# Two VectorE instructions of a softmax joined into one scalar_tensor_tensor, under a list scheduler

## The chip, the cores and the metric

The kernel runs on the 8 cores of one Trainium2 chip. Cores work in pairs on one of four sequences; nothing passes between them on the chip. The metric is the device time of the slowest core in microseconds. Each core has TensorE (PE: matmuls), VectorE (DVE), ScalarE (ACT), GpSimd (POOL) and SyncE (SP: issues transfers here). A transfer is a DMA.

## What is computed

`x` has the shape 4 x 4096 x 1024. The reference, cut to its core:

```
def attn(x):                       # x is layernormed
    out = gelu(x); on = out / |out|
    sim = on @ on.T, strictly causal, max over the past
    fam = w * max_sim + (1 - w) * (on @ ema)
    gate = 1 - alpha + alpha * exp(-tau * fam)
    return out * gate[..., None]

def ffn(x):                        # x is layernormed, tokens n
    gate = softmax(xt @ gate_w.T, axis=-1)                    # 8 experts
    base = xt @ weight.T                                      # 1024 x 1024
    t = einsum('nh,erh->ner', xt, lora_U)                     # rank 16
    lora = einsum('ne,eor,ner->no', gate, lora_V, t)
    return base + lora / 16

x = x + attn(layernorm(x))
x = x + ffn(layernorm(x))
```

## The kernel before

Each core owns 16 tiles of 128 tokens (`NSLOT`) and sees 32 key tiles. Three stages overlap in time.

The key stage loads tiles, takes mean and variance, applies gelu (L422) and the norm, makes the normalised tile in bf16 (L446, GpSimd), transposes it on TensorE (L455) into two PSUM banks and casts both halves into `kT` (L461 on VectorE, L465 on ScalarE). The similarity stage (`qk_slot`) multiplies one own tile with blocks of up to 512 keys (L507), two blocks at a time, and VectorE takes the maximum of each block (L528). The third stage is the feed-forward one. For tile `m` it holds, in `g_slot` and the two functions that the print below shows:

- `g_slot`: gating and residual (L612), statistics (L618, L619, L621), and two ScalarE steps for the inverse deviation (L623, L627).
- `ffn_part1`: L643 and L647 make the layernormed tile `z2tok`; L657 transposes it; L664 (VectorE) and L667 (ScalarE) cast the halves into `kT`. Then L678 and L681 make, over 8 chunks, the low-rank product (128 columns) and the gate's logits (8 columns) in one bank. L684 and L687 make the big product, 16 matmuls of 512 columns into two banks. The softmax runs over L694 (maximum), L697 (exponential, on ScalarE), L701 (sum), L704 (reciprocal), L707 (scaling the 8 exponentials) and L710 (the low-rank product times the 8 gates, each over 16 columns, into `tgb`).
- `ffn_part2`: L721 transposes `tgb`, L725 (ScalarE) copies it, L728 and L730 add the low-rank part to the big product, L733 and L736 add the result to `h`. Two tiles at a time are written out from SyncE's queue.

PSUM has eight banks: `ps0` to `ps4` go round for L507, L684 and L687 (two for each tile), `ps6` and `ps7` for the transposes (L455, L657, L721), and `ps5` alone is for L678 and L681 of every tile:

```
    pspools = {"big": [0, 1, 2, 3, 4], "tr": [6, 7], "one": [5]}
```

No engine's order is written out. `P.op` records operations with what they read and write, and a cost in ns. `P.schedule` is a list scheduler: an operation's priority is its cost plus the largest priority of those that need its result, and at each step the operation that can start earliest by these costs is taken, the higher priority first. So the costs set the order of each engine's instructions and nothing else:

```
            o.prio = o.cost + o.bonus + m
...
                if best is None or st < best[0] or \
                        (st == best[0] and nprio < best[1]):
                    best = (st, nprio, e, oid)
```

Of the kernel before, what the change touches and what calls it, by code (L numbers as in the profile page):

```python
# [12 lines left out]
ALU = mybir.AluOpType  # L13
# [190 lines left out]
def build_program():  # L204
# [57 lines left out]
    rinv2 = sb("rinv2", [128, 2], F32)  # L262
    gexp2 = sb("gexp2", [128, 2, 8], F32)
# [10 lines left out]
    def psalloc(pool="big"):  # L274
        lst = pspools[pool]
        i = lst[psidx[pool] % len(lst)]
        psidx[pool] += 1
        return pst[i], ("ps", i)
# [9 lines left out]
    p = P()  # L288
# [8 lines left out]
         reads=[("ident",)], writes=[("identf",)], cost=200.0)  # L297
# [3 lines left out]
         writes=[("xbuf", 1)], dma=True)  # L301
# [3 lines left out]
         reads=[("srow",)], writes=[("crow",)])  # L305
    p.op("scalar", lambda e: e.activation(crow[:, 5:6], srow[:, 1:2], AF.Exp, scale=-1.0),
         reads=[("srow",)], writes=[("crow",)])
    p.op("scalar", lambda e: e.activation(crow[:, 6:7], srow[:, 2:3], AF.Exp, scale=-1.0),
         reads=[("srow",)], writes=[("crow",)])
    p.op("vector", lambda e: e.tensor_scalar(crow[:, 5:6], crow[:, 5:6], 1.0, None, ALU.add),  # L310
         reads=[("crow",)], writes=[("crow",)])
    p.op("vector", lambda e: e.reciprocal(crow[:, 2:3], crow[:, 5:6]),
         reads=[("crow",)], writes=[("crow",)])
    p.op("vector", lambda e: e.tensor_scalar(crow[:, 3:4], crow[:, 2:3], -1.0, 1.0, ALU.mult, ALU.add),
         reads=[("crow",)], writes=[("crow",)])
    p.op("vector", lambda e: e.tensor_scalar(crow[:, 6:7], crow[:, 6:7], 1.0, None, ALU.add),
         reads=[("crow",)], writes=[("crow",)])
    p.op("vector", lambda e: e.reciprocal(crow[:, 7:8], crow[:, 6:7]),
         reads=[("crow",)], writes=[("crow",)])
    p.op("vector", lambda e: e.tensor_tensor(crow[:, 0:1], crow[:, 4:5], crow[:, 7:8], ALU.mult),  # L320
         reads=[("crow",)], writes=[("crow",)])
    p.op("vector", lambda e: e.tensor_scalar(crow[:, 6:7], crow[:, 7:8], -1.0, 1.0, ALU.mult, ALU.add),
         reads=[("crow",)], writes=[("crow",)])
    p.op("vector", lambda e: e.tensor_tensor(crow[:, 1:2], crow[:, 4:5], crow[:, 6:7], ALU.mult),
         reads=[("crow",)], writes=[("crow",)])
# [4 lines left out]
         reads=[("ones",), ("crow",)], writes=[tC])  # L330
    p.op("vector", lambda e: e.tensor_copy(constcols[:, :], psC[:, 0:8]),
         reads=[tC], writes=[("constcols",)])
# [7 lines left out]
         reads=[("zt", 0)], writes=[("xbuf", 0), ("tiny",)])  # L340
    p.op("vector", lambda e: e.tensor_scalar(tiny[:, 0:1], tiny[:, 0:1], 1e-24, None, ALU.max),
         reads=[("tiny",)], writes=[("tiny",)])
    p.op("scalar", lambda e: e.activation(tiny[:, 1:2], tiny[:, 0:1], AF.Ln),
         reads=[("tiny",)], writes=[("tiny",)])
    p.op("scalar", lambda e: e.activation(tiny[:, 2:3], tiny[:, 1:2], AF.Exp, scale=-0.5),
         reads=[("tiny",)], writes=[("tiny",)])
    p.op("vector", lambda e: e.tensor_scalar(embf, emarow, tiny[:, 2:3], None, ALU.mult),
         reads=[("zt", 0), ("tiny",)], writes=[("ktok", 0)])
    psE, tE = psalloc("big")
    fns = []  # L350
    for c in range(NCHUNK):
# [5 lines left out]
         reads=[tE], writes=[("emaf",)])  # L357

    p.op("vector", lambda e: e.tensor_copy(gwbf, wstage[0:8, 1, :]),
         reads=[("xbuf", 1)], writes=[("ktok", 1)])  # L360
    psG, tG = psalloc("big")
    fns = []
    for c in range(NCHUNK):
# [7 lines left out]
        reads=[tG], writes=[("gwTb",)])  # L371

    p.default_bonus = 0.0
    for c in range(NCHUNK):
        p.op("scalar", lambda e, c=c: e.dma_start(
            wstage[:, c % 2, :], wtd[c * 128:(c + 1) * 128, :]),
            writes=[("xbuf", c % 2)], dma=True, cost=2500.0)
        p.op("vector", lambda e, c=c: e.tensor_copy(wTb[:, c, :], wstage[:, c % 2, :]),
             reads=[("xbuf", c % 2)], writes=[("wTb",)], cost=600.0)
# [3 lines left out]
        writes=[("xbuf", 0)], dma=True)  # L383
    p.op("vector", lambda e: e.tensor_copy(
        uTb[:, :, :], wstage[:, 0, :].rearrange("p (c j) -> p c j", c=8)),
        reads=[("xbuf", 0)], writes=[("uTb",)])
    p.op("scalar", lambda e: e.dma_start(wstage[:, 1, :], vpd),
         writes=[("xbuf", 1)], dma=True)
    p.op("vector", lambda e: e.tensor_scalar(vPb[:, :], wstage[:, 1, :], 0.0625, None, ALU.mult),
         reads=[("xbuf", 1)], writes=[("vPb",)])  # L390
# [250 lines left out]
    def ffn_part1(m):  # L641
        buf = m % 2
        p.op("vector", lambda e: e.scalar_tensor_tensor(  # L643
            rtmp16[:, m:m + 1], mv2[:, m, 0:1], -1.0, rstd16[:, m:m + 1],
            ALU.mult, ALU.mult),
            reads=[("mv2", m), ("rstd16", m)], writes=[("rtmp16", m)], cost=90.0)
        p.op("scalar", lambda e: e.activation(  # L647
            z2tok[:, buf, :], h[:, m, :], AF.Identity,
            bias=rtmp16[:, m:m + 1], scale=rstd16[:, m:m + 1]),
            reads=[("h", m), ("rtmp16", m), ("rstd16", m)], writes=[("z2", buf)],  # L650
            cost=700.0, act_set="lnexp")
        pa, ta = psalloc("tr")
        pb, tb = psalloc("tr")
        fns = []
        for c in range(NCHUNK):
            ps = pa if c < 4 else pb
            fns.append(lambda e, c=c, ps=ps: e.matmul(  # L657
                ps[:, (c % 4) * 128:(c % 4) * 128 + 128],
                z2tok[:, buf, c * 128:(c + 1) * 128], ident[:, :],
                start=(c % 4 == 0), stop=(c % 4 == 3), skip_group_check=True))  # L660
        p.op("tensor", fns, reads=[("z2", buf), ("ident",)], writes=[ta, tb],
             cost=900.0)
        col = 128 * m
        p.op("vector", lambda e: e.tensor_copy(  # L664
            kT[:, 0:4, col:col + 128], pa[:, :].rearrange("p (c f) -> p c f", c=4)),
            reads=[ta], writes=[("kT", m, 0)], cost=660.0)
        p.op("scalar", lambda e: e.copy(  # L667
            kT[:, 4:8, col:col + 128], pb[:, :].rearrange("p (c f) -> p c f", c=4)),
            reads=[tb], writes=[("kT", m, 1)], cost=580.0)
        z2toks = [("kT", m, 0), ("kT", m, 1)]  # L670
        psA, tA = psalloc("big")
        psB, tB = psalloc("big")
        psT, tT = psalloc("one")
        fnsT = []
        fnsAB = []
        for c in range(NCHUNK):
            lhs = kT[:, c, 128 * m:128 * m + 128]
            fnsT.append(lambda e, c=c, lhs=lhs, psT=psT: e.matmul(  # L678
                psT[:, 0:128], lhs, uTb[:, c, :],
                start=(c == 0), stop=(c == 7), skip_group_check=True))  # L680
            fnsT.append(lambda e, c=c, lhs=lhs, psT=psT: e.matmul(  # L681
                psT[:, 128:136], lhs, gwTb[:, c, :],
                start=False, stop=(c == 7), skip_group_check=True))
            fnsAB.append(lambda e, c=c, lhs=lhs, psA=psA: e.matmul(  # L684
                psA[:, :], lhs, wTb[:, c, 0:512],
                start=(c == 0), stop=False, skip_group_check=True))
            fnsAB.append(lambda e, c=c, lhs=lhs, psB=psB: e.matmul(  # L687
                psB[:, :], lhs, wTb[:, c, 512:1024],
                start=(c == 0), stop=False, skip_group_check=True))
        p.op("tensor", fnsT, reads=z2toks + [("uTb",), ("gwTb",)],  # L690
             writes=[tT], cost=1350.0)
        p.op("tensor", fnsAB, reads=z2toks + [("wTb",)],
             writes=[tA, tB], cost=3550.0)
        p.op("vector", lambda e, psT=psT: e.reduce_max(  # L694
            nmax2[:, buf:buf + 1], psT[:, 128:136], axis=AX, negate=True),
            reads=[tT], writes=[("nmax", buf)])
        p.op("scalar", lambda e, psT=psT: e.activation(  # L697
            gexp2[:, buf, :], psT[:, 128:136], AF.Exp, bias=nmax2[:, buf:buf + 1]),
            reads=[tT, ("nmax", buf)], writes=[("gexp", buf)],
            cost=310.0, act_set="lnexp")  # L700
        p.op("vector", lambda e: e.reduce_sum(  # L701
            ssum2[:, buf:buf + 1], gexp2[:, buf, :], axis=AX),
            reads=[("gexp", buf)], writes=[("ssum", buf)])
        p.op("vector", lambda e: e.reciprocal(  # L704
            rinv2[:, buf:buf + 1], ssum2[:, buf:buf + 1]),
            reads=[("ssum", buf)], writes=[("rinv", buf)])
        p.op("vector", lambda e: e.tensor_scalar(  # L707
            gexp2[:, buf, :], gexp2[:, buf, :], rinv2[:, buf:buf + 1], None, ALU.mult),
            reads=[("gexp", buf), ("rinv", buf)], writes=[("gexp", buf)])
        p.op("vector", lambda e, psT=psT: e.tensor_tensor(  # L710
            tgb[:, buf, :].rearrange("p (ee r) -> p ee r", ee=8),
            psT[:, 0:128].rearrange("p (ee r) -> p ee r", ee=8),
            gexp2[:, buf, :].unsqueeze(2).broadcast_to([128, 8, 16]),
            ALU.mult),
            reads=[tT, ("gexp", buf)], writes=[("tg", buf)], cost=280.0)
        return (m, buf, psA, tA, psB, tB, psT, tT)

    def ffn_part2(st):
# [28 lines left out]
    for m in range(NSLOT):  # L747
        st = ffn_part1(m)
        if prev is not None:
            ffn_part2(prev)  # L750
        prev = st
# [55 lines left out]
```

How the kernel before makes its waits and increments, by code:

```python
                def section(eng, ename=ename):  # L172
                    clk = {}
                    for oid in self.sched[ename]:
                        o = ops[oid]
                        waits = {}
                        for pid in o.preds:
                            p_ = ops[pid]
                            if clk.get(p_.semn, 0) < p_.semv:
                                if waits.get(p_.semn, 0) < p_.semv:
                                    waits[p_.semn] = p_.semv
                        if o.dma and o.semv > 16:
                            prev = o.semv - 16
                            if clk.get(o.semn, 0) < prev and \
                                    waits.get(o.semn, 0) < prev:
                                waits[o.semn] = prev
                        for s, v in sorted(waits.items()):
                            eng.wait_ge(sems[s], v)
                            if clk.get(s, 0) < v:
                                clk[s] = v
                        inst = None
                        for fn in o.fns:
                            inst = fn(eng)
                        if inst is not None:
                            inst.then_inc(sems[o.semn], 16 if o.dma else 1)
                    if ename == "gpsimd":
                        for s in QPOOL["sync"] + QPOOL["scalar"]:
                            if totals.get(s, 0) > 0:
                                eng.wait_ge(sems[s], totals[s])
```

## Time and profile before

| | us |
|---|---|
| time before, median of 2 runs | 391.79 (391.3 to 392.28) |
| the profiled execution | 392.92 |
| its span on the slowest core (core 1) | 391.3 |
| spans of the eight cores | 385.0 to 391.3 |
| busy in the span: PE / DVE / ACT / POOL | 244.5 / 236.9 / 148.0 / 60.7 |

The span runs from the first to the last instruction of a core. The profiled execution's own time stands 1.6 us above the span. Busy times of engines overlap, so they don't add up to the span. The mean granted clock of TensorE was 0.946 of full speed on this core and 0.945 to 0.950 on the others.

### The profile page before, as it was taken

Reading aid. Unit: us, or ns where it says so; the run is one execution under the profiler, and the core shown is the slowest. Engines: PE = TensorE matmul, PEld = TensorE weight load, DVE = VectorE, ACT = ScalarE, POOL = GpSimd, SP = SyncE. Lnnn points to the kernel's source line nnn. Section 1 sums busy time; section 2 is a strip of 40 time slices with the busy share of each in tenths; the row PEclk is TensorE's granted clock in tenths of the full one; section 3 lists DMA queues with packets and bytes.
Section 4 is the critical chain, followed back from the end, with each engine's and each line's share of the span. In section 5 each row is a group of like instructions: output and inputs, shape, how many; then the busy total and the mean of one; then the engine's idle time right before and its main releaser. Section 6 shows DMA issues by size and latency. Waiting matters only on the chain.

```text
span 391.3 us, 5559 instructions; the slowest of 8 cores (385.0 to 391.3 us)
## 1 busy us (share of the span) xinstructions
PE 244.5 (62%) x1762; PEld 135.1 (35%) x1762; DVE 236.9 (61%) x537; ACT 148.0 (38%) x252; POOL 60.7 (16%) x38
## 2 busy tenths in 40 slices
PE   0100000166567777788588797889879688887781
PEld 0000000064234444455234354445445344443540
DVE  0222177755857677648634656459889796877533
ACT  1100009755665571731731065103354344243410
POOL 0000000563242325115013013210000000000000
PEclk9999999999688899999969999999989999999895
DMA  7866510236033333113303030333330222022222
GB/s 218 281 201 182 133 73 0 107 107 216 1 107 109 111 107 108 54 55 109 107 2 107 1 109 1 109 107 110 107 108 7 104 110 107 6 104 107 109 110 108
DMA packets 11665, 39.30 MB, mean 100 GB/s; under 512 B 1259, under 2 KB 2283, under 8 KB 11636
## 3 DMA queue, kind: packets, MB, share of 16 engines
q1 hardware_dynamic: 6528, 25.17, 18.2%
q10 hardware_dynamic: 5108, 13.78, 11.1%
q8 instruction: 15, 0.25, 0.2%
q14 instruction: 14, 0.11, 0.1%
HBM read 30.55 MB, written 8.39 MB: 100 GB/s over the span
## 4 chain that ended last, share of the span: by engine, by line
PE 37%; DVE 21%; issue 15%; ACT 12%; DMA 11%; DVEq 1%; ACTq 0%; SPq 0%
PE ps L507 22%; DMA xbuf<-wt 4%; PE ps L455 3%; PE ps L684 3%; PE ps L687 3%; ACT xbuf L422 3%; DVE st L411 3%; ACT h L422 2%; DVE colbuf L528 2%; ACT L422 2%; PE ps L678 2%; PE ps L657 2%; DMA ztile<-ema 2%; DMA xbuf<-x 2%; DMA xbuf<-gw 2%
## 5 line engine op out<-in xcount | busy, mean ns | idle before, releaser
L507 PE MATMUL ps<-kT 128*128 128x512 bf16 (+3 forms) x640 | 136.7, 368 | 24.0 <-DVE colbuf L528 9.2
L507 PEld LDWEIGHTS ps<-kT 128*128 128x128 bf16 x640 | 53.7, 102 | 72.3 <-issue 34.2
L455 PE MATMUL ps<-identb,ktok 128*128 128x128 bf16 x256 | 22.7, 241 | 76.6 <-POOL ktok L446 51.8
L528 DVE TENSOR_REDUCE colbuf<-ps 128x1 f32<-128x512 f32 (+3 forms) x80 | 47.5, 602 | 27.6 <-PE ps L514 15.6
L446 POOL TENSOR_TENSOR ktok<-h,inv 128x1024 bf16<-128x1024 f32 x16 | 30.3, 1892 | 136.4 <-ACT rtmp L545 67.9
L684 PE MATMUL ps<-wTb,kT 128*128 128x512 bf16 x128 | 49.3, 385 | 1.7 <-DVE rinv L704 1.0
L687 PE MATMUL ps<-wTb,kT 128*128 128x512 bf16 x128 | 49.0, 383 | 0.0
L465 ACT CAST kT<-ps 128x512 bf16<-128x512 f32 x32 | 18.5, 579 | 74.3 <-PE ps L455 74.2
L455 PEld LDWEIGHTS ps<-identb,ktok 128*128 128x128 bf16 x256 | 17.9, 108 | 79.7 <-issue 78.7
L461 DVE CAST kT<-ps 128x512 bf16<-128x512 f32 x32 | 22.0, 686 | 33.2 <-PE ps L455 33.2
L446 POOL TENSOR_TENSOR ktok<-xbuf,inv 128x1024 bf16<-128x1024 f32 x16 | 30.3, 1892 | 57.3 <-PE ps L455 57.3
L647 ACT ACTIVATE z2tok<-h,rtmp,rstd 128x1024 bf16<-128x1024 f32 x16 | 19.9, 1241 | 16.6 <-DVE rtmp L643 16.6
L410 DVE BATCH_NORM_STATS2 st<-xbuf 128x6 f32<-128x512 f32 x32 | 21.7, 678 | 6.3 <-DMA xbuf<-x 6.3
L545 ACT ACTIVATE rtmp<-mvg,constf 128x4 f32<-128x4 f32 x8 | 2.4, 295 | 58.3 <-DVE mvg L413 52.7
L514 PE MATMUL ps<-emaf,kT 128*128 128x1 bf16 x128 | 22.2, 174 | 0.0
L411 DVE BATCH_NORM_STATS2 st<-xbuf 128x6 f32<-128x512 f32 x32 | 21.6, 675 | 0.0
L612 DVE SCALAR_TENSOR_TENSOR h<-h,gate,xbuf 128x1024 f32<-128x1024 f32 x16 | 20.2, 1265 | 1.0 <-DVE mv L621 0.5
L422 ACT ACTIVATE xbuf<-xbuf,mb,rstd 128x1024 f32<-128x1024 f32 x16 | 19.7, 1234 | 0.1
L422 ACT ACTIVATE h<-xbuf,mb,rstd 128x1024 f32<-128x1024 f32 x16 | 19.6, 1228 | 0.0
L434 DVE SCALAR_TENSOR_TENSOR xbuf<-h 128x1024 f32<-128x1024 f32 x8 | 12.3, 1535 | 11.8 <-ACT h L422 11.8
L514 PEld LDWEIGHTS ps<-emaf,kT 128*128 128x128 bf16 x128 | 13.7, 107 | 15.3 <-issue 3.6
L684 PEld LDWEIGHTS ps<-wTb,kT 128*128 128x128 bf16 x128 | 12.7, 99 | 17.3 <-issue 4.1
(98 smaller groups left out, 307.0 us busy)
## 6 DMA issues: line engine op xcount, KB each, us to landing
xbuf<-x SPq DMA_DIRECT2D x16, 1024.0 KB, 5.2
xbuf<-x ACTq DMA_DIRECT2D x8, 1024.0 KB, 4.9
y<-h SPq DMA_DIRECT2D x8, 1024.0 KB, 4.0
xbuf<-wt ACTq DMA_DIRECT2D x8, 512.0 KB, 4.3
xbuf<-ut ACTq DMA_DIRECT2D x1, 512.0 KB
xbuf<-vp ACTq DMA_DIRECT2D x1, 512.0 KB
xbuf<-gw ACTq DMA_DIRECT2D x1, 32.0 KB
identb<-ident ACTq DMA_DIRECT2D x1, 32.0 KB, 7.0
```

The source lines that it names most:

```text
L410: lambda e: e.bn_stats(st6[:, g2, i, 0:6], xbuf[:, ri, 0:512]),
L411: lambda e: e.bn_stats(st6[:, g2, i, 6:12], xbuf[:, ri, 512:1024]),
L422: p.op("scalar", lambda e: e.activation(gdst, xbuf[:, ri, :], AF.Gelu_apprx_tanh, bias=mb8[:, g2, i:i + 1], scale=rstd8[:, g2, i:i + 1]), ...
L446: p.op("gpsimd", lambda e: e.tensor_tensor(ktok[:, buf, :], gdst, inv8[:, g2, i:i + 1].broadcast_to([128, D]), ALU.mult), reads=[gtok, ("i ...
L455: fns.append(lambda e, c=c, ps=ps: e.matmul(ps[:, (c % 4) * 128:(c % 4) * 128 + 128], ktok[:, buf, c * 128:(c + 1) * 128], ident[:, :], st ...
L461: p.op("vector", lambda e: e.tensor_copy(kT[:, 0:4, col:col + 128], pa[:, :].rearrange("p (c f) -> p c f", c=4)), reads=[ta], writes=[("kT ...
L507: fns.append(lambda e, c=c, pt=pts[bi], off=off, W=W, iswin=iswin: e.matmul(pt[:, 0:W], kT[:, c, 128 * m:128 * m + 128], kT[:, c, off:off ...
L514: fns.append(lambda e, c=c, pe_t=pe_t: e.matmul(pe_t[:, 0:1], kT[:, c, 128 * m:128 * m + 128], emaf[:, c:c + 1], start=(c == 0), stop=(c = ...
L528: p.op("vector", lambda e, pt=pts[bi], W=W, ci=cb_idx: e.reduce_max(colbuf[:, cbuf, ci:ci + 1], pt[:, 0:W], axis=AX), reads=[ptoks[bi]], w ...
L612: p.op("vector", lambda e, m=m, i=i: e.scalar_tensor_tensor(h[:, m, :], h[:, m, :], gate16[:, m:m + 1], xbuf[:, i, :], ALU.mult, ALU.add), ...
L684: fnsAB.append(lambda e, c=c, lhs=lhs, psA=psA: e.matmul(psA[:, :], lhs, wTb[:, c, 0:512], start=(c == 0), stop=False, skip_group_check=True))
L687: fnsAB.append(lambda e, c=c, lhs=lhs, psB=psB: e.matmul(psB[:, :], lhs, wTb[:, c, 512:1024], start=(c == 0), stop=False, skip_group_check ...
```

## The change

L707 and L710 become one instruction. Before, the 8 exponentials of a token were scaled by the reciprocal of their sum, and the result was multiplied into the 128 low-rank values. Afterwards a single scalar_tensor_tensor multiplies the 128 values by the reciprocal (one column, `rinv2`) and by the exponentials. The costs in the list are 150 (the default) and 280 before, and 280 after; so one operation of 150 is missing from it for each tile.

```
-        p.op("vector", lambda e: e.tensor_scalar(
-            gexp2[:, buf, :], gexp2[:, buf, :], rinv2[:, buf:buf + 1], None, ALU.mult),
-            reads=[("gexp", buf), ("rinv", buf)], writes=[("gexp", buf)])
-        p.op("vector", lambda e, psT=psT: e.tensor_tensor(
+        p.op("vector", lambda e, psT=psT: e.scalar_tensor_tensor(
             tgb[:, buf, :].rearrange("p (ee r) -> p ee r", ee=8),
             psT[:, 0:128].rearrange("p (ee r) -> p ee r", ee=8),
+            rinv2[:, buf:buf + 1],
             gexp2[:, buf, :].unsqueeze(2).broadcast_to([128, 8, 16]),
-            ALU.mult),
-            reads=[tT, ("gexp", buf)], writes=[("tg", buf)], cost=280.0)
+            ALU.mult, ALU.mult),
+            reads=[tT, ("gexp", buf), ("rinv", buf)], writes=[("tg", buf)],
+            cost=280.0)
```

In the changed file the joined instruction is L707, and lines behind it are one lower (L720 for L721, L727 for L728, L732 for L733, L735 for L736).

The scheduler makes another order of it, from similarity tile 14 to the end. Three places follow. TensorE, the pair of tiles 6 and 7, before: the first row is the big product of tile 6, `ps5` is the bank of L678, `ps2` the big product of tile 7.

```order
L684 MATMUL ps0<-wTb,kT 128x512
...
L678 MATMUL ps5<-uTb,kT 128x128
...
L721 MATMUL ps6<-identb,tgb 128x128
L684 MATMUL ps2<-wTb,kT 128x512
...
L657 MATMUL ps7<-identb,z2tok 128x128 x4
L657 MATMUL ps6<-identb,z2tok 128x128 x4
L678 MATMUL ps5<-uTb,kT 128x128
```

The same pair afterwards, from the big product of tile 6 on:

```order
L684 MATMUL ps0<-wTb,kT 128x512
...
L684 MATMUL ps2<-wTb,kT 128x512
...
L678 MATMUL ps5<-uTb,kT 128x128
...
L720 MATMUL ps6<-identb,tgb 128x128
L657 MATMUL ps7<-identb,z2tok 128x128 x4
L657 MATMUL ps6<-identb,z2tok 128x128 x4
L727 MATMUL ps0<-vPb,tgTb 128x512
L729 MATMUL ps1<-vPb,tgTb 128x512
L678 MATMUL ps5<-uTb,kT 128x128
```

L678 of tile 7 and L678 of tile 8 had the big product of tile 7 between them; now that product stands ahead of both. The pairs from 0/1 to 10/11 read like this one now. The pair 12/13 had both products ahead of L678 already, and there L721 of tile 13 stands ahead of L678 of tile 14, before and afterwards.

VectorE, the softmax of tile 7, before:

```order
L694 TENSOR_REDUCE nmax2<-ps5 128x1
L621 BN_AGGR mv2<-st26 128x2
L612 SCALAR_TENSOR_TENSOR h<-h,gate16,xbuf 128x1024
L701 TENSOR_REDUCE ssum2<-gexp2 128x1
L704 RECIPROCAL rinv2<-ssum2 128x1
L707 TENSOR_SCALAR gexp2<-gexp2,rinv2 128x8
L710 TENSOR_TENSOR tgb<-ps5,gexp2 128x128
```

And afterwards:

```order
L694 TENSOR_REDUCE nmax2<-ps5 128x1
L621 BN_AGGR mv2<-st26 128x2
L600 TENSOR_SCALAR gate16<-gate16,constcols 128x4
L612 SCALAR_TENSOR_TENSOR h<-h,gate16,xbuf 128x1024
L664 CAST kT<-ps7 128x4x128
L701 TENSOR_REDUCE ssum2<-gexp2 128x1
L704 RECIPROCAL rinv2<-ssum2 128x1
L707 SCALAR_TENSOR_TENSOR tgb<-ps5,rinv2,gexp2 128x128
```

L664, the cast of tile 8, now stands between the maximum and the sum.

TensorE, the last blocks of similarity tile 14 (`ps1` to `ps4`) and the transpose of key tile 30 (L455), before:

```order
L521 MATMUL ps0<-maskmb,identb 128x128
L455 MATMUL ps6<-identb,ktok 128x128 x4
L455 MATMUL ps7<-identb,ktok 128x128 x4
L507 MATMUL ps1<-kT 128x512
...
L507 MATMUL ps3<-kT 128x512
```

And afterwards:

```order
L521 MATMUL ps0<-maskmb,identb 128x128
L507 MATMUL ps1<-kT 128x512
...
L455 MATMUL ps6<-identb,ktok 128x128 x4
L455 MATMUL ps7<-identb,ktok 128x128 x4
L507 MATMUL ps3<-kT 128x512
```

The blocks in `ps3` and `ps4`, which read key tile 30, now come right behind its transpose.

## Rows read from the trace of the kernel before

**Rows 1.** The page: busy tenths and clock in 40 slices; the chain by engine.

```profile
PE   0100000166567777788588797889879688887781
...
DVE  0222177755857677648634656459889796877533
...
PEclk9999999999688899999969999999989999999895
...
PE 37%; DVE 21%; issue 15%; ACT 12%; DMA 11%; DVEq 1%; ACTq 0%; SPq 0%
```

**Rows 2.** TensorE's timeline, big products of tiles 2 and 12 (start, duration, ...).

```profile
294.45 0.38 PE L684 MATMUL ps<-wTb,kT 128*128 128x512 bf16 x1
...
358.74 0.38 PE L684 MATMUL ps<-wTb,kT 128*128 128x512 bf16 x1
```

**Rows 3.** Timeline of TensorE, after the big products of tiles 12 and 13.

```profile
365.64 0.22 PE L678 MATMUL ps<-uTb,kT 128*128 128x128 bf16 x1
...
367.12 0.61 PE L657 MATMUL ps<-identb,z2tok 128*128 128x128 bf16 x8 [0.61 <-ACT gexp L697]
...
369.59 0.26 PE L721 MATMUL ps<-identb,tgb 128*128 128x128 bf16 x1 [1.43 <-DVE tgb L710]
369.71 0.27 PE L678 MATMUL ps<-uTb,kT 128*128 128x128 bf16 x1
```

**Rows 4.** Timeline of VectorE, the softmax of tile 13.

```profile
367.18 0.16 DVE L701 TENSOR_REDUCE ssum<-gexp 128x1 f32<-128x8 f32 x1 [0.46 <-ACT gexp L697]
367.83 0.69 DVE L664 CAST kT<-ps 128x512 bf16<-128x512 f32 x1 [0.50 <-PE ps L657]
368.44 0.15 DVE L704 RECIPROCAL rinv<-ssum 128x1 f32<-128x1 f32 x1
368.70 0.23 DVE L707 TENSOR_SCALAR gexp<-gexp,rinv 128x8 f32<-128x8 f32 x1
369.04 0.29 DVE L710 TENSOR_TENSOR tgb<-ps,gexp 128x128 bf16<-128x128 f32 x1
```

**Rows 5.** VectorE's groups by line from 262 us (count, busy us, mean ns).

```profile
L612 DVE SCALAR_TENSOR_TENSOR h<-h,gate,xbuf 128x1024 f32<-128x1024 f32 x16 | 20.2, 1265 | 1.0 <-DVE mv L621 0.5 <-DVE gate L600 0.3
...
L710 DVE TENSOR_TENSOR tgb<-ps,gexp 128x128 bf16<-128x128 f32 x16 | 4.6, 290 | 1.5
L707 DVE TENSOR_SCALAR gexp<-gexp,rinv 128x8 f32<-128x8 f32 x16 | 3.7, 230 | 1.2
...
L643 DVE SCALAR_TENSOR_TENSOR rtmp<-mv,rstd 128x1 f32<-128x1 f32 x16 | 2.4, 151 | 0.6 <-ACT rstd L627 0.6
...
L594 DVE SCALAR_TENSOR_TENSOR gtmp<-ecol,constcols,gtmp 128x4 f32<-128x4 f32 x4 | 0.9, 222 | 0.5
```

**Rows 6.** Timeline of TensorE, pair 8/9: five starts, tile 8 to tile 10.

```profile
333.20 0.38 PE L684 MATMUL ps<-wTb,kT 128*128 128x512 bf16 x1 [0.62 <-DVE h L733]
...
336.65 0.22 PE L678 MATMUL ps<-uTb,kT 128*128 128x128 bf16 x1
...
343.19 0.22 PE L678 MATMUL ps<-uTb,kT 128*128 128x128 bf16 x1 [1.00 <-DVE kT L664]
...
344.82 0.61 PE L657 MATMUL ps<-identb,z2tok 128*128 128x128 bf16 x8 [0.33 <-ACT gexp L697]
...
345.69 0.38 PE L684 MATMUL ps<-wTb,kT 128*128 128x512 bf16 x1
```

**Rows 7.** Stretches: length; busy PE, PEld, DVE, ACT, POOL; clock; DMA.

```profile
276.40:294.45 18.05, 13.94 (x129) 8.22 (x128) 15.06 (x41) 7.48 (x16) 0.00 (x0) 0.91 0.35 117
284.00:287.20 3.20, 2.65 (x13) 1.58 (x14) 3.09 (x9) 2.11 (x5) 0.00 (x0) 0.50 0.02 5
311.00:312.60 1.60, 0.04 (x2) 0.05 (x2) 1.03 (x2) 1.32 (x2) 0.00 (x0) 1.00 0.00 0
369.25:372.65 3.40, 3.06 (x28) 2.46 (x29) 1.37 (x3) 0.85 (x2) 0.00 (x0) 0.51 0.00 0
```

**Rows 8.** Timeline of TensorE, behind L455 of key tile 15.

```profile
261.39 0.38 PE L507 MATMUL ps<-kT 128*128 128x512 bf16 x1 [1.08 <-DVE kT L461]
```

## The prediction

> **What bounds the kernel now.** I read the slices of the page first. From about 264 to 303 us (slices 28 to 31), where the last similarity tiles and the first feed-forward tiles meet, VectorE's tenths are 9, 8, 8, 9; behind that they move between 9 and 5 and end at 3. TensorE's are 8 and 7 there and up to 9, and its matmul records overlap, so that this is not its peak. The granted clock is at its upper level (2.4 GHz) nearly everywhere and dips in a few slices. The chain that ended last says the same: TensorE 37%, VectorE 21%, "issue" 15%, ScalarE 12% of the span; no engine carries it alone [rows 1]. The changed line lies only in the feed-forward stage, so the rest of the reading is there. Its 16 tiles are done in pairs. From the first matmul of tile 2's big product (294.45) to that of tile 12 (358.74) five pairs pass in 64.29 us, 12.86 us each [rows 2]. A pair's two big products take 6.90 us (tile 12's starts at 358.74, tile 13's is over when L678 starts at 365.64) [rows 2, 3]. What remains is a chain of short steps over three engines, and TensorE waits in it.
>
> **What the edit itself takes out.** Sixteen L707 instructions go, each 230 ns long [rows 4, 5]. In the one place that I follow closely L707 starts at 368.70 and L710 at 369.04: 0.34 us from start to start, which is what the chain loses with it [rows 4]. The new L707 does L710's work with a column as scalar. L710 takes 290 ns [rows 5]. The trace has no scalar_tensor_tensor on 128 columns of PSUM with a column scalar, so I bound it. Below: no dearer than L710, 0.29 us. Above: L594, with a column scalar and 4 columns, takes 222 ns, and L643, with one element and a constant, 151 ns, so a column scalar may add 0.07 us [rows 5]. I take 0.36 us, since L594 has the same kind of operands. Net: 0.34 - 0.07 = 0.27 us for a tile, 16 x 0.27 = 4.3 us for the kernel, if every one of them lies on the path; without the 0.07 it is 5.4 us, off the path it is 0.
>
> The row shows 230 ns and 0.34 us for an L707 that works on 8 elements [rows 4, 5]. The Trainium skill, "VectorE: DVE Perf Modes", section "The TRN2 errata", prices a VectorE instruction from SBUF to SBUF at 58 cycles and one for each element; an estimate from that page is 66 cycles at 0.96 GHz, 69 ns, and 16 of them would be 1.1 us. By the page the whole edit could bring hardly more than a microsecond; the trace's duration is over three times that, and I keep to the trace. The same page's section "Rules for kernel authors" says not to fuse chained VectorE operations for speed and to minimise their number; here both happen at once, and the row prices the one instruction that goes.
>
> **What moves with it.** The list scheduler works from costs. The removed operation counted 150 in it, so priorities and start times behind it change, and so does the order, from similarity tile 14 on. This is the larger part of the change. It moves no DMA of the SP queue; on ScalarE's queue the loads of L608 shift by one or two instructions, and none of them is waited for in this stage, so I cost them at nothing (if one came late, L612 would wait for it).
>
> *Feed-forward pairs.* Before, from tile 5 to tile 13 at least one big product lies between any two neighbouring L678 (the low-rank and gate product); only those of tiles 2/3, 4/5 and 13/14 stand side by side. Afterwards every pair from 0/1 on has both big products first, then L678 of the odd tile, and L678 of the next even tile soon behind. All L678 write the one bank ps5, so the next must wait until the softmax of the last is through with it. With a big product between, 3.45 us of it hide that softmax; side by side nothing does. The pair 12/13 of before is the new arrangement, measured: L678 of tile 13 at 365.64, L657 of tile 14 at 367.12 (1.48 later), and tile 13's scaled product ready for L721 at 369.59, 3.95 us after L678; L678 of tile 14 follows at 369.71 [rows 3]. Pair 8/9 is the old arrangement: L678 of tile 9 at 336.65 is hidden, and L678 of tile 10 starts at 343.19, 9.99 us after the pair's start at 333.20 [rows 6].
>
> Does the removed instruction shorten the 3.95? Before, L701 and the cast L664 run at 367.18 and 367.83, then L704 at 368.44, L707 at 368.70, L710 at 369.04 [rows 4]. Afterwards L701 stands behind L664: it starts at about 368.44, L704 0.26 later and the fused L707 0.26 behind that, at about 369.0. The 0.34 saved is taken back by the two that now stand behind the cast. So L678 of the next even tile starts 3.95 after that of the odd one. The rest of a pair: L678 to L657 again 1.48 us (L721, its copy on ScalarE, L657), and from L657 over L728 and L730 to the next big product 0.87 us (344.82 to 345.69) [rows 6]. Sum: 6.90 + 3.95 + 1.48 + 0.87 = 13.20 us, against 12.86. Five pairs: 5 x 0.34 = 1.7 us lost. In the pair 6/7 an L612 of 1.27 us [rows 5] now stands ahead of L664 and L701 as well; beside L664's own wait it costs about 0.4. The bounds of this term: 0, if ScalarE's copy or the next cast is quicker than in these rows, and 5 x 0.86 = 4.3 us (10.85 - 9.99 up to L678 of the even tile, nothing won back after it).
>
> *The clock.* The same waits let it fall. In pair 12/13 the clock was at 0.51 in 369.25 to 372.65, behind two waits; at 284.00 to 287.20 it was 0.50, at 311.00 to 312.60, with TensorE busy for 0.04 us only, it stayed at 1.00 [rows 7]. So of the seven pair changes two show a fall, and the one with the new arrangement is among them. A fall costs at most half of its 3.4 us, 1.6, of which part lies in waits anyway; I take 1.0. Afterwards all pair changes have that arrangement, but for one L721 behind its L678 instead of ahead of it. I take one fall more than before, +1.0 us; the bounds are 0 and five more at 1.6, 8.0 us.
>
> *The start of the stage.* L455 of key tile 30 now stands behind a block of L507, right ahead of the block that reads its keys. Before, a whole block lay between. The nearest row is L455 of tile 15, directly ahead of its reader: TensorE waits 1.08 us for the cast [rows 8]. VectorE is later by that 1.1 us and by the gate arithmetic (L582, L584), which stood in a wait and now doesn't: about 1.7 us at L612 of tile 0. From 276.40 to 294.45 VectorE is busy for 15.06 of 18.05 us [rows 7]: 3.0 us of idle time can take most of it in, and two or three removed L707 give 0.3 each. Between 0 and 1.7 I take 0.6.
>
> *The end.* L678 of tile 15, its softmax and the last additions are in the same order; the chain there is shorter by 0.27 us.
>
> **Sum.** 1.7 + 0.4 + 1.0 + 0.6 - 0.3 = +3.4 us. The profiled execution took 392.92 us, with a span of 391.3 and 1.6 around it; the median is 391.79, and the shares that I add don't depend on which of them I take. I forecast 391.8 + 3.4 = 395.2 us. A measurement of this kernel can tell about 2%, 7.8 us, from no change, so that is "the same".
>
> **Rivals.**
> (1) *The saving reaches the path.* If TensorE waits for VectorE wherever a softmax is open, each tile gives its 0.27 us and the new order costs nothing: 391.8 - 4.3 = 387.5. For it: VectorE at 8 to 9 tenths as the stage begins [rows 1]. Against it: in the old order a big product already hid every second softmax, and the cast L664 now stands ahead of L701.
> (2) *The order is neutral.* The longer pair and the shorter start cancel; 390.5 to 393.5.
> (3) *Slower by over 2%: the clock falls at every pair change.* Place: behind L678 of the odd tile, where TensorE has three waits close together. Price: up to 1.6 us a fall, five more falls, 8.0, on top of the 2.4 of order, start and end: 402.2; at 1.0 each 399.2. It decides from four more falls on. For it: the one pair of before with exactly this arrangement fell. Against: in the wait at 311.00 to 312.60 it did not [rows 7].
> (4) *The change does nothing.* It would, if VectorE ran the fused instruction slower than both together (0.57 us): 392 to 393. The rows of L594 and L643 speak against it.
>
> **Chances.** Forecast (393.5 to 398): 0.45. Rival 1, with all between 386 and 390.5: 0.2. Rivals 2 and 4: 0.2. Rival 3, from 398 up: 0.15, most of it above 399.6. The range 388 to 401 leaves out the lower half of rival 1 and the upper end of rival 3. Faster by over 2% (under 384.0) would need more than the whole saving: 0.03. Slower by over 2%: 0.13. Within: 0.84.
>
> **What would show it.** The fused L707 at 0.29 to 0.36 us. Big products of even tiles 13.2 us apart, and L678 of the even tile 3.9 us behind that of the odd one, released by the fused L707. A wait of about 1.1 us ahead of the last block of tile 14. More slices with a clock at 0.5 behind 295 us than one. I would be wrong if L678 of the even tile starts earlier than that (then ScalarE and the cast, not the softmax, set it), if the first feed-forward tiles start 2 us or more later than before, or if the clock falls in every pair.

## The result

| | us |
|---|---|
| before, median (10 runs) | 393.28 |
| the changed kernel, median (11 runs) | 406.66 |
| ratio, 95% interval | 1.0342, 1.0318 to 1.0367 |
| the changed kernel's profiled execution; its span on the slowest core (core 5) | 406.13; 404.3 |
| spans of its eight cores | 398.3 to 404.3 |

The medians take in runs in which a die was disturbed; the ratio is of undisturbed runs alone. The change makes the kernel 3.4% slower, some 13 us. The forecast was 3.4 us more, and the time lies outside its range of 388 to 401.

The page of the changed kernel: busy tenths of TensorE and VectorE, the granted clock, and the chain's shares by engine, as in [rows 1].

```profile
PE   0000000283647878789488878797887886977891
...
DVE  0322197646777568558346563488867976883343
...
PEclk9999999999778899899699999998969969969997
...
PE 46%; DVE 18%; ACT 13%; issue 11%; DMA 10%; DVEq 1%; ACTq 0%; SPq 0%
```

VectorE is less full than before behind slice 28 and TensorE's share of the chain is up from 37% to 46%. From slice 28 on the clock's row reads 8, 9, 6, 9, 9, 6, 9, 9, 6, 9, 9, 9, 7; before it was 9 there but for 8, 8 and 5. Three slices ahead of the last one read 6 now; before, none of these read below 8. The joined instruction itself, in VectorE's groups from 262 us on:

```profile
L707 DVE SCALAR_TENSOR_TENSOR tgb<-ps,rinv,gexp 128x128 bf16<-128x128 f32 x16 | 5.6, 351 | 1.8
```

It takes 0.35 us, as costed (290 ns, and 0.07 for the column scalar). So the instruction isn't what is dear.

Where the 13.0 us between the two spans lie:

| stretch (first matmuls) | before | after | difference |
|---|---|---|---|
| start to L678 of tile 0 | 276.40 | 280.51 | +4.1 |
| to the big product of tile 2 | 18.05 | 18.04 | 0.0 |
| tile 2 to tile 12, five pairs | 64.29 | 75.52 | +11.2 |
| tile 12 to tile 14 | 13.70 | 12.54 | -1.2 |
| tile 14 to the end of the span | 18.86 | 17.69 | -1.2 |

(Before: L678 of tile 0 starts at 276.40, where the first stretch of [rows 7] begins; 294.45 and 358.74 are in [rows 2]; tile 14's product begins at 372.44. After: 280.51, 298.55, 374.07 and 386.61.) The last two rows are shorter by more than the joined instruction can give. Before, the clock was low from 369.3 to 372.7, in the fourth stretch, and again for the last 8.4 us of the span; the changed kernel has no fall in the fourth stretch and a low clock for the last 4.2 us alone. The start, on VectorE and on TensorE:

```profile
278.49 1.27 DVE L612 SCALAR_TENSOR_TENSOR h<-h,gate,xbuf 128x1024 f32<-128x1024 f32 x1
279.69 0.68 DVE L664 CAST kT<-ps 128x512 bf16<-128x512 f32 x1
```

```profile
280.51 0.22 PE L678 MATMUL ps<-uTb,kT 128*128 128x128 bf16 x1 [2.79 <-DVE kT L664]
...
298.55 0.63 PE L684 MATMUL ps<-wTb,kT 128*128 128x512 bf16 x1
```

L664, the cast for tile 0, stands behind L612 and starts at 279.69; TensorE waited 2.79 us for it, and as the wait ended, at 280.6, the clock fell. Tile 0's transposes (L657) have moved as well: before they ran at 272.45, ahead of the last similarity blocks, and now they run at 277.11, behind them. The blocks themselves end only 0.7 us later than before (277.05 against 276.35). A pair change that ran as the prediction has it, that of tiles 10/11 to 12/13. TensorE: L678 of tile 11, L657 of tile 12, L678 of tile 12, the big product of tile 12.

```profile
367.88 0.22 PE L678 MATMUL ps<-uTb,kT 128*128 128x128 bf16 x1
...
369.36 0.61 PE L657 MATMUL ps<-identb,z2tok 128*128 128x128 bf16 x8 [0.61 <-ACT gexp L697]
...
371.71 0.22 PE L678 MATMUL ps<-uTb,kT 128*128 128x128 bf16 x1 [1.31 <-DVE tgb L707]
...
374.07 0.38 PE L684 MATMUL ps<-wTb,kT 128*128 128x512 bf16 x1
```

VectorE in between: cast of tile 12, sum, reciprocal and joined product of tile 11.

```profile
370.08 0.69 DVE L664 CAST kT<-ps 128x512 bf16<-128x512 f32 x1 [1.12 <-PE ps L657]
370.69 0.15 DVE L701 TENSOR_REDUCE ssum<-gexp 128x1 f32<-128x8 f32 x1
370.94 0.16 DVE L704 RECIPROCAL rinv<-ssum 128x1 f32<-128x1 f32 x1
371.22 0.35 DVE L707 SCALAR_TENSOR_TENSOR tgb<-ps,rinv,gexp 128x128 bf16<-128x128 f32 x1
```

L678 of the even tile comes 3.83 us behind that of the odd one (the forecast was 3.95), L657 of the even tile 1.48 behind that same L678 of the odd one, and from L678 of tile 12 to the product it takes 2.36 (forecast 1.48 + 0.87 = 2.35). With 6.90 that is 13.1 us. But the five pairs took 14.34, 15.30, 16.24, 15.03 and 14.61. What is added shows in stretches (length; busy PE, PEld, DVE, ACT, POOL; clock), to set beside [rows 7]:

```profile
281.50:284.00 2.50, 2.50 (x16) 1.44 (x13) 1.93 (x6) 1.12 (x4) 0.00 (x0) 0.50 0.92 370
294.00:301.00 7.00, 5.44 (x33) 3.23 (x34) 3.91 (x14) 1.31 (x5) 0.00 (x0) 0.52 0.28 110
325.00:332.00 7.00, 6.39 (x35) 3.31 (x32) 4.27 (x12) 2.26 (x4) 0.00 (x0) 0.51 0.01 2
342.00:345.50 3.50, 2.89 (x17) 1.61 (x15) 1.56 (x4) 1.02 (x3) 0.00 (x0) 0.51 0.00 0
355.50:362.50 7.00, 6.04 (x35) 3.44 (x36) 5.41 (x13) 2.40 (x5) 0.00 (x0) 0.51 0.01 2
```

These are five falls of the clock in this stage where before had two. The rows are cut at round times; the clock was low from 280.6 to 284.0, 294.3 to 301.1, 325.0 to 331.8, 342.0 to 345.5 and 355.7 to 362.5, together 27.3 us against 6.8 before. Three of them last 6.8 us instead of 3.4. Why these last longer isn't shown: a later wait of 0.61 us lies inside each of the three, but one lies inside the short fall at 342.0 too. In the same execution cores 4 and 7 had four falls and 17.1 us of low clock; theirs are the two shortest spans, 401.2 and 398.3 us.

### The profile page after: what moved, and what is told of

It reads as the page before. It is cut to its first block, busy times and chain, and to the rows that moved or that the text cites. A ratio compares the mean times of both kernels' runs of the same rounds, so it can differ in the third digit from the quotient of the medians.

```text
span 404.3 us, 5527 instructions; the slowest of 8 cores (398.3 to 404.3 us)
## 1 busy us (share of the span) xinstructions
PE 252.5 (62%) x1762; PEld 139.3 (34%) x1762; DVE 236.0 (58%) x521; ACT 147.8 (37%) x252; POOL 60.7 (15%) x38
## 4 chain that ended last, share of the span: by engine, by line
PE 46%; DVE 18%; ACT 13%; issue 11%; DMA 10%; DVEq 1%; ACTq 0%; SPq 0%
PE ps L507 23%; PE ps L684 6%; PE ps L687 6%; DMA xbuf<-wt 4%; PE ps L455 3%; ACT xbuf L422 3%; PE ps L678 3%; DVE st L411 3%; ACT h L422 3%; PE ps L657 2%; DVE colbuf L528 2%; ACT L422 2%; DMA identb<-ident 2%; DVE kT L461 2%; DVE h L612 2%
## 5 line engine op out<-in xcount | busy, mean ns | idle before, releaser
L455 PE MATMUL ps<-identb,ktok 128*128 128x128 bf16 x256 | 22.6, 240 | 77.1 <-POOL ktok L446 51.0
L528 DVE TENSOR_REDUCE colbuf<-ps 128x1 f32<-128x512 f32 (+3 forms) x80 | 47.5, 603 | 26.5 <-PE ps L514 15.6
L684 PE MATMUL ps<-wTb,kT 128*128 128x512 bf16 x128 | 52.3, 408 | 0.0
L687 PE MATMUL ps<-wTb,kT 128*128 128x512 bf16 x128 | 51.8, 404 | 0.0
L446 POOL TENSOR_TENSOR ktok<-h,inv 128x1024 bf16<-128x1024 f32 x16 | 30.3, 1892 | 136.7 <-ACT rtmp L545 66.9
L455 PEld LDWEIGHTS ps<-identb,ktok 128*128 128x128 bf16 x256 | 17.9, 108 | 80.2 <-issue 79.1
L446 POOL TENSOR_TENSOR ktok<-xbuf,inv 128x1024 bf16<-128x1024 f32 x16 | 30.3, 1892 | 60.5 <-PE ps L455 60.5
L647 ACT ACTIVATE z2tok<-h,rtmp,rstd 128x1024 bf16<-128x1024 f32 x16 | 19.8, 1240 | 11.8 <-DVE rtmp L643 11.4
L678 PE MATMUL ps<-uTb,kT 128*128 128x128 bf16 x128 | 14.0, 228 | 12.4 <-DVE tgb L707 6.2
L612 DVE SCALAR_TENSOR_TENSOR h<-h,gate,xbuf 128x1024 f32<-128x1024 f32 x16 | 20.4, 1276 | 1.0 <-DVE gate L600 1.0
L684 PEld LDWEIGHTS ps<-wTb,kT 128*128 128x128 bf16 x128 | 13.5, 106 | 17.9 <-issue 5.3
L687 PEld LDWEIGHTS ps<-wTb,kT 128*128 128x128 bf16 x128 | 13.4, 105 | 17.6 <-issue 4.7
```

What stands on the lines that cost most here:

```text
L446: p.op("gpsimd", lambda e: e.tensor_tensor(ktok[:, buf, :], gdst, inv8[:, g2, i:i + 1].broadcast_to([128, D]), ALU.mult), reads=[gtok, ("i ...
L455: fns.append(lambda e, c=c, ps=ps: e.matmul(ps[:, (c % 4) * 128:(c % 4) * 128 + 128], ktok[:, buf, c * 128:(c + 1) * 128], ident[:, :], st ...
L528: p.op("vector", lambda e, pt=pts[bi], W=W, ci=cb_idx: e.reduce_max(colbuf[:, cbuf, ci:ci + 1], pt[:, 0:W], axis=AX), reads=[ptoks[bi]], w ...
L612: p.op("vector", lambda e, m=m, i=i: e.scalar_tensor_tensor(h[:, m, :], h[:, m, :], gate16[:, m:m + 1], xbuf[:, i, :], ALU.mult, ALU.add), ...
L678: fnsT.append(lambda e, c=c, lhs=lhs, psT=psT: e.matmul(psT[:, 0:128], lhs, uTb[:, c, :], start=(c == 0), stop=(c == 7), skip_group_check= ...
L684: fnsAB.append(lambda e, c=c, lhs=lhs, psA=psA: e.matmul(psA[:, :], lhs, wTb[:, c, 0:512], start=(c == 0), stop=False, skip_group_check=True))
```

## The experiments

Theory A: the order does it. The parts of this theory: (A1) two L678 side by side expose a softmax and (A1b) the cast ahead of the sum lengthens it, (A2) the clock falls in the waits, (A3) the stage starts later. Rival B: the joined instruction does it. All times are medians, with the ratio to runs of the kernel before on the same chip.

**e1_joined_old_order.** The old operation stays in the schedule, without an instruction; those that needed it take over what it needed. Every engine then has the order of before.

```
         p.op("vector", [],
              reads=[("gexp", buf), ("rinv", buf)], writes=[("gexp", buf)])
         p.op("vector", lambda e, psT=psT: e.scalar_tensor_tensor(
...
def edit_order(p):
    ghosts = {o.oid for o in p.ops if not o.fns}
    for o in p.ops:
        for g in [x for x in o.preds if x in ghosts]:
            o.preds.discard(g)
            o.preds |= p.ops[g].preds
    for e in ENGINES:
        p.sched[e] = [x for x in p.sched[e] if x not in ghosts]
```

> The joined instruction, with every engine's order exactly that of the kernel before (the removed operation still counts in the schedule and issues nothing). Theory A (the new order costs the time, the instruction itself is cheap): 388 to 393 us, the fused instruction at 0.29 to 0.36 us, big products of tiles 2 and 12 at most 64.3 us apart. Rival B (the joined instruction is dear, or holds PSUM longer than both did): 400 us or more, with an instruction well over 0.57 us.

Measured: 391.84 us, ratio 0.9966 (0.9953 to 0.9979). The joined instruction:

```profile
L709 DVE SCALAR_TENSOR_TENSOR tgb<-ps,rinv,gexp 128x128 bf16<-128x128 f32 x16 | 5.6, 348 | 1.0
```

0.35 us and no loss: theory A. The big products of tiles 2 and 12 are 63.93 us apart, against 64.29 before. Of the 4.3 us that could be won at most, 1.3 arrive. This run also has one fall of the clock more than the kernel before, three against two (at 284.9, 356.6 and 370.3, 3.4 us each), which takes up to 1.7 us off the gain.

**e2_apart_new_order.** The kernel before with one number:

```
-            reads=[("gexp", buf), ("rinv", buf)], writes=[("gexp", buf)])
+            reads=[("gexp", buf), ("rinv", buf)], writes=[("gexp", buf)], cost=0.0)
```

> Both instructions as before, but the scaling counts 0 in the schedule instead of 150, which gives exactly the order of the changed kernel on every engine. Theory A: the time of the changed kernel or up to 4 us above it, 405 to 411 us. Rival B: about 393 us, since the instructions are those of before.

Measured: 411.71 us, ratio 1.0479 (1.0462 to 1.0495). The instructions of before, in the order of the changed kernel, lose 4.8%: rival B falls. The time is 5 us above that of the changed kernel, 0.7 above the range that was expected. Here is the whole stretch from L678 of tile 1 to that of tile 13, in this run and then in the changed kernel:

```profile
289.60:385.50 95.90, 76.23 (x517) 41.35 (x516) 64.93 (x162) 32.37 (x74) 0.00 (x0) 0.82 0.20 77
```

```profile
290.08:380.97 90.89, 72.77 (x517) 39.49 (x516) 62.60 (x150) 32.38 (x74) 0.00 (x0) 0.87 0.21 82
```

95.90 us at a mean clock of 0.82 against 90.89 at 0.87. In this order the joined instruction is worth 5 us by the medians, more than its own 4.3 us. The clock has a share in it: its slowest core has eight falls in the stage here, 41 us of low clock, against five and 27.3 us.

**e3_apart.** The changed kernel, with moves of operations after scheduling (`(a, b)`: a right ahead of b on its engine). In this and the following cuts of code some of the comments are added for the reader:

```
+    for m in range(1, 13, 2):
+        p.moves.append((p.tag["T", m], p.tag["AB", m]))       # L678 ahead of L684
+        for x in ("sum", "rinv", "tg"):                       # L701, L704, L707
+            p.moves.append((p.tag[x, m], p.tag["cast", m + 1]))   # ahead of L664
```

> The changed kernel with one move in each of the six pairs 0/1 to 10/11: L678 of the odd tile back between the two big products, and its sum, reciprocal and joined product ahead of the next even tile's cast on VectorE. Theory A1 (the softmax is exposed because two L678 stand side by side): a pair goes back from 15.1 us to 12.5 to 13, five pairs give some 11 us, 395 to 399 us; the later start of the stage (4 us) stays. Rival (the start of the stage, or the whole order, is the cause and not these pairs): 403 us or more.

Measured: 402.35 us, ratio 1.0241 (1.022 to 1.0262). Some 4 us come back, not 11: between the two expectations. From the first matmul of one even tile's big product to that of the next it took 12.39 us between tiles 10 and 12, less than the 12.86 of before, and there TensorE waited 0.62 us ahead of L678; but in the four pairs ahead it took 13.9 to 15.0. TensorE at one of them, L657 and L678 of tile 6:

```profile
319.89 0.61 PE L657 MATMUL ps<-identb,z2tok 128*128 128x128 bf16 x8 [0.78 <-ACT tgTb L724]
...
323.18 0.22 PE L678 MATMUL ps<-uTb,kT 128*128 128x128 bf16 x1 [2.25 <-DVE kT L664]
```

And VectorE, which holds it up:

```profile
320.35 1.28 DVE L612 SCALAR_TENSOR_TENSOR h<-h,gate,xbuf 128x1024 f32<-128x1024 f32 x1
321.55 0.15 DVE L701 TENSOR_REDUCE ssum<-gexp 128x1 f32<-128x8 f32 x1
```

L612 of a later tile stands between the maximum and the sum of tile 5, so the softmax is late in spite of its cover, and the clock fell there (324.4 to 327.8) too. What stands ahead of L701 on VectorE exposes the softmax even under a big product. Whether two L678 side by side cost anything by themselves this run can't tell, since it moves L678 and the softmax together; e6_cast_later can.

**e4_fill.** The changed kernel's order, with matmuls of no use in the waits; `fill` writes them into the bank of the next even tile's big product, which overwrites them with `start=True`:

```
+        for target, n in ((("tr", m), 2), (("T", m), 5), (("tr", m + 1), 2)):
+            fill(m, target, n)      # n matmuls ahead of L657, L678, the next L657; even m from 2 on
```

> The changed kernel with nine extra matmuls of 512 columns in each pair change (two ahead of L657, five ahead of the even tile's L678, two ahead of the odd tile's L657), into the bank of the next big product, which overwrites them. They stand in the waits and keep TensorE busy there; no other order is changed. Theory A2 (the clock falls in these waits, and that costs most of the time): no fall behind 295 us, big products at 6.9 us for a pair, 398 to 402 us. Rival (the waits cost, the clock doesn't): 406 us or more, since the extra matmuls themselves may come up to 0.3 us late at each place.

Measured: 400.26 us, ratio 1.0187 (1.0169 to 1.0205). From L678 of tile 1 to that of tile 13:

```profile
290.90:373.20 82.30, 74.20 (x560) 38.97 (x570) 62.24 (x150) 32.30 (x74) 0.00 (x0) 1.00 0.23 90
```

82.30 us at full clock (2.4 GHz), with nine matmuls more in each pair change, against 90.89 at 0.87. This is the price of the clock, less what the extra matmuls themselves hold up: 8.6 us in this stretch, 6.4 us by the medians. Part of the difference between the two lies behind the stretch, where the clock fell for good 8 us before the end of this run and 4.2 us before the end of the changed kernel. Up to there its last fall is the one at 281.4, ahead of the first extra matmul. Theory A2 holds in that the clock no longer falls; by the medians it is about half of the loss, not most of it.

**e5_start.**

```
+    p.moves.append((p.tag["ktr", 30], p.tag["qk", 14, 2]))     # L455 of key tile 30
+    p.moves.append((p.tag["kcast", 30], p.tag["max", 14, 4]))  # where it stood
+    p.moves.append((p.tag["cast", 0], p.tag["stats", 2]))      # L664 of tile 0
```

> The changed kernel with three moves at the start of the stage and none behind: L455 of key tile 30 ahead of a block of L507 again, its cast ahead of that block's maximum (where it stood), and L664 of tile 0 ahead of the statistics of tile 2 on VectorE. Theory A3 (4 us of the loss arise because the first L678 waits for a cast that stands behind 3 us of statistics and gating): L678 of tile 0 at 277 to 278 us instead of 280.5, 402 to 404 us; less than that if one clock fall goes too. Rival (the start is made up later, VectorE is the bound there): 405 to 407 us.

Measured: 404.95 us, ratio 1.0292 (1.0262 to 1.0322), 1.7 us better than the changed kernel by the medians, with intervals that just overlap, and just below the rival's lower end. TensorE, L678 of tile 0, then L657 and L678 of tile 2:

```profile
276.12 0.22 PE L678 MATMUL ps<-uTb,kT 128*128 128x128 bf16 x1 [0.94 <-DVE kT L664]
...
289.52 0.96 PE L657 MATMUL ps<-identb,z2tok 128*128 128x128 bf16 x8 [4.54 <-ACT gexp L697]
...
292.22 0.27 PE L678 MATMUL ps<-uTb,kT 128*128 128x128 bf16 x1 [0.88 <-DVE tgb L707]
```

L678 of tile 0 starts at 276.12, as early as before (276.40). (This execution is 1.4 us ahead of the other two long before the moves: GpSimd starts the same L446 at 239.33, in both others at 240.69. Allowing for that, L678 is 3.0 us earlier than in the changed kernel and 1.1 later than before.) But ahead of L657 of tile 2 TensorE now waits 4.54 us, and the product of tile 2 starts at 295.8. From 283.94 to 289.78 VectorE works through two L612, two pairs of L618/L619 and a maximum (L528), and tile 1's L694 stands in the midst of them. Of the 3.0 us that L678 of tile 0 wins, 1.4 are left at the product of tile 2, with the same allowance. So the first L678 alone was not what bounded the start; the gating work in VectorE's queue holds it up next. What is left of the gain isn't a clean price of the start either, since the slowest core has six falls of the clock in the stage here, 34 us, against five and 27.3 us.

**e6_cast_later.** Only the inner loop of e3_apart: TensorE's order stays that of the changed kernel.

> The changed kernel with TensorE's order untouched; on VectorE the odd tile's sum, reciprocal and joined product stand ahead of the next even tile's cast (L664) in the pairs 0/1 to 10/11. If the cast in front of the sum sets when the next L678 may start, L678 of the even tile comes 3.2 us behind that of the odd one instead of 3.83 to 4.9, six times 0.7 us: 401 to 403.5 us. If it is the softmax with the product side by side whatever the order on VectorE, or the gating ahead of both: 405 to 407 us.

Measured: 401.97 us, ratio 1.0211 (1.0183 to 1.0239), the time that was expected for the first case, though only part of its reason holds. TensorE, L678 of tiles 11 and 12, and VectorE, the sum of tile 11 and the cast of tile 12:

```profile
364.31 0.22 PE L678 MATMUL ps<-uTb,kT 128*128 128x128 bf16 x1
...
367.48 0.22 PE L678 MATMUL ps<-uTb,kT 128*128 128x128 bf16 x1 [0.65 <-DVE kT L664]
```

```profile
365.84 0.16 DVE L701 TENSOR_REDUCE ssum<-gexp 128x1 f32<-128x8 f32 x1 [0.46 <-ACT gexp L697]
...
366.65 0.68 DVE L664 CAST kT<-ps 128x512 bf16<-128x512 f32 x1
```

3.17 us from L678 to L678 instead of 3.83. But it does so at three of the six pair changes only: at 1/2, 3/4 and 11/12 the distance shrinks by 0.5, 0.6 and 0.7 us, at 5/6, 7/8 and 9/10 not at all (4.94, 4.42 and 4.01). TensorE, L678 of tiles 5 and 6:

```profile
319.09 0.22 PE L678 MATMUL ps<-uTb,kT 128*128 128x128 bf16 x1
...
324.03 0.22 PE L678 MATMUL ps<-uTb,kT 128*128 128x128 bf16 x1 [2.25 <-DVE kT L664]
```

So the moves themselves give 1.7 us, not six times 0.7. The gain by the medians is 4.7 us; with it the low clock of the stage went from 27.3 to 20.5 us (four falls, that of pair 9/10 gone and that of 5/6 half as long). The time is that of e3_apart within the intervals. And it settles what e3_apart left open: from the product of tile 10 to that of tile 12 it takes 12.43 us here (12.39 there), less than the 12.86 of before, with the two L678 still side by side. Once the softmax stands ahead of the cast, a big product between the two wins nothing more.

**e7_old_order_fill.** e1_joined_old_order with extra matmuls ahead of eleven operations; for each tile the lines list ahead of what and how many (`tr` is L657, `T` is L678, `tt` is L721):

```
+    1: [(("tr", 2), 7)], 5: [(("tr", 6), 5)], 6: [(("tr", 7), 2)], 8: [(("T", 8), 4), (("tr", 9), 2)],
+    10: [(("tr", 10), 2), (("T", 10), 4)], 12: [(("tr", 12), 5), (("T", 12), 4)],
+    14: [(("tr", 14), 2), (("tt", 13), 6)]}
```

> The joined instruction in the order of before (as in e1_joined_old_order) with extra matmuls of 512 columns in its longest waits, so that the clock doesn't fall there: 388 to 390.5 us if the three falls of that run (5.1 us of lost clock) cost what they look like, 391 to 393 us if they lie in waits anyway or the extra matmuls come late.

Measured: 390.08 us, ratio 0.9916 (0.9886 to 0.9947), as expected for the first case. The stage from 276 to 381 us:

```profile
276.00:381.00 105.00, 93.62 (x701) 48.91 (x699) 76.60 (x188) 39.43 (x90) 0.00 (x0) 0.98 0.24 91
```

This is the best version of the study: 0.8% below the kernel before. Its interval lies below that of e1_joined_old_order, 0.5% better; in this stage one fall is left of three (at 289.3).

**e8_all_moves.** The moves of e3_apart and e5_start, and:

```
+    for m, g in ((5, 10), (7, 12)):
+        for x in (("sum", m), ("rinv", m), ("tg", m), ("cast", m + 1)):
+            p.moves.append((p.tag[x], p.tag["gate", g]))       # ahead of L612 of tile g
```

> The changed kernel with the moves of e3_apart and e5_start together, and in the pairs 4/5 and 6/7 the odd tile's softmax and the next cast ahead of an L612 of a later tile, which held them up by 1.3 to 2.2 us in e3_apart. If these three are the whole of the cause, the time is back at 391 to 395 us. If the parts don't add up (the clock falls elsewhere): 397 us or more.

Measured: 395.95 us, ratio 1.0061 (1.004 to 1.0082). The stage, from 276 to 386 us:

```profile
276.00:386.00 110.00, 88.61 (x687) 47.92 (x684) 79.65 (x192) 39.92 (x94) 0.00 (x0) 0.95 0.23 87
```

Of the 13 us some 11 are back by moves of some thirty operations past their neighbours, and three falls of the clock are left. 2.4 us above the kernel before remain, between the two expectations.

**e9_cost_430.** The changed kernel with one number:

```
-            cost=280.0)
+            cost=430.0)
```

> The changed kernel with one number changed: the joined operation counts 430 in the schedule (150 + 280, as the two did) instead of 280. The order is then nearly that of before: on TensorE two neighbouring operations are exchanged (L684 of tile 5 and L657 of tile 6), on VectorE ten places differ, on ScalarE three. Theory A (the order is the cause, and it hangs on the cost that the list is given): 390 to 394 us, as e1_joined_old_order. Rival (any departure from the order of before is dear, since it was a lucky one): 397 us or more.

Measured: 391.64 us, ratio 0.9968 (0.9951 to 0.9984), as theory A has it. One number of the cost table makes the difference between 3.4% slower and 0.3% faster.

## Why the prediction was wrong

**The instruction.** Right: 0.36 us forecast, 0.35 measured. In the order of before 1.3 of the possible 4.3 us arrive, 0.08 us a tile. That a big product hides most of the softmaxes there fits this, but the one fall more of that run has a part in it that wasn't taken apart. The prediction's estimate from the Trainium skill, "VectorE: DVE Perf Modes", section "The TRN2 errata", was 1.1 us for the whole edit, near to these 1.3, but not for its reason: the removed instruction is 230 ns long, not 69, and in the order of the change it was worth 5 us.

**The mechanism of the pairs.** Right in its chain: the bank `ps5`, the cast ahead of the sum. 3.95 us were forecast, 3.83 measured at the two pair changes without other work in between (3/4 and 11/12), and e6_cast_later took 0.6 to 0.7 off there. Half wrong in the cause: with two L678 side by side nothing hides the softmax, as the prediction says, but that isn't what makes the pair longer than before, since with the softmax ahead of the cast a pair with its L678 side by side took 12.43 us.

**The term of the pairs was too small.** Forecast 1.7 + 0.4. In e4_fill, at full clock, L678 of tile 3 started at 305.07 and that of tile 13 at 373.25: 13.64 us for each of five pairs, against 12.86. That is 3.9 us, at most, since the extra matmuls hold up some L678 by up to 0.4 us. The step that failed is "In the pair 6/7 an L612 now stands ahead": I costed one place, at 0.4. In the changed kernel L678 of the even tile came 4.93, 4.42 and 4.00 us behind at 5/6, 7/8 and 9/10, so three changes are late by VectorE's or ScalarE's other work, by 1.1, 0.6 and 0.2 us. With 5 x (13.09 - 12.86) for the clean part that makes 3.0 us, so the term was 3.0 to 3.9 us where 2.1 were forecast. (The waits just ahead of those L678 are put down to the joined product, to L627 and to L647.)

**The term of the clock was the gross error.** "I take one fall more than before, +1.0 us": there were five against two in the stage, two of them of 3.4 us and three of 6.8. Of the 11.2 us of the five pairs at least 11.2 - 3.9 = 7.3 are the clock's by this run's profile, and by the medians filling the waits gives back 6.4 us. Two steps failed. One is the count and the length: three falls more than before and not one, and three of the five twice as long as the rows of before had it, so that the low clock grew from 6.8 to 27.3 us. The other is that a fall costs 1.0 us, since part of it lies in waits. In the five low stretches of the changed kernel (2.5 + 7 + 7 + 3.5 + 7 = 27.0 us) TensorE is busy for 2.50 + 5.44 + 6.39 + 2.89 + 6.04 = 23.3 us, so nearly all of a low stretch is work at half speed, and little of it a wait. (The prediction put half of 3.4 us at 1.6; it is 1.7.) The range failed with this term: the upper bounds that the prediction gives its terms, 4.3, 0.4, 8.0 and 1.7, add up to 14.4 us, and its range ends at 9.

**The start.** Forecast 0.6 (0 to 1.7), and 4.1 us by the first L678. The wait that was costed is there, 1.13 us at 257.91 for the cast of key tile 30. What was put at nothing without a reason is tile 0's own chain: its transposes now stand behind the last similarity blocks and its cast behind an L612, and of the 4.1 us some 3.4 arise there. "3.0 us of idle time can take most of it in" failed too: the stretch up to tile 2's product took 18.04 us, against 18.05, with the clock at 0.79 instead of 0.91. e5_start shows that this L678 isn't the only bound: 3.0 us earlier, it left 1.4 us at that product.

**The end.** Forecast -0.3; from tile 12's product on it was -2.4. This goes with the clock: the fall of before behind the pair 12/13, which the forecast took to stay, is gone, though the order there is the same, and the low clock at the end is 4.2 us shorter.

**The rivals.** Rival 3, slower by the clock falling at the pair changes, comes nearest to what happened: 402.2 as its upper price, of which 8.0 were the clock's. It had 0.15. It didn't come as stated: the clock fell at four of the seven pair changes and at the start, three falls more than before, where the rival wanted four; the three long ones made up for it. The rows of before could not settle it. The pair 12/13 with the new arrangement fell, and I weighed it against a wait at 311 us that did not, though that was another arrangement; but the L678 of 2/3 and 4/5 of before stood side by side too, and the clock stayed up behind them.

**What stays open.** Why the clock fell at some pair changes and not at others with nearly the same waits (9/10 did, with 0.61, 1.49 and 0.61 us; 3/4 and 11/12 did not, with 0.61, 1.31 and 0.61; 13/14 did before and does not now) isn't settled; in one execution of the changed kernel six cores have five falls and two have four. Nor is it settled why some falls last twice as long, or which part of the last 2.4 us in e8_all_moves is order and which clock.

## What to carry to other kernels

Where a list scheduler makes the order, a change of one cost is a change of the whole order. Build the changed instruction in the old order first (a joined instruction gets the cost of both that it replaces), and take the new order as a change of its own; only then does a time say anything about the instruction. When short waits on TensorE are moved close together, cost the clock with them: work behind such waits at half speed was more than the waits themselves here. Put an operation that frees a single buffer ahead of casts and statistics on its engine that don't need it: here that brought 4.7 us, part of it by the clock.

## What the runs showed of the hardware

- Matmuls that nobody needs made the kernel faster: nine of 512 columns in each pair change took the stretch from 90.89 to 82.30 us, with the granted clock at 1.00 instead of 0.87, and the kernel from 406.66 to 400.26 us.
- A saving on VectorE of 0.27 us a tile was worth 1.3 us in one order (ratio 0.9966) and 5 us in another (406.66 against 411.71 us). The falls of the clock changed with it: on the slowest cores, from two to three in the first order and from eight to five in the second.
- A scalar_tensor_tensor on 128 columns of PSUM with a column as scalar took 0.35 us, against 0.29 us for the tensor_tensor without it.
